# Fused image network with a deformable convolution: two of nine taps of image 1 sampled densely on TensorE instead of gathered

## The reference, cut to what matters

```python
y0 = jnp.floor(y); x0 = jnp.floor(x)      # y, x: base position of the tap plus its offset
val = w00 * gather(y0i, x0i) + w01 * gather(y0i, x1i) + w10 * gather(y1i, x0i) + w11 * gather(y1i, x1i)
val = val * msk                            # zero outside the image
out = jnp.einsum('op,bphw->bohw', weight, col)   # 32 outputs from 9 taps x 32 channels
```

## Time and profile before

| what | us |
|---|---|
| median of 3 runs | 1137.83 |
| lowest, highest | 1137.09, 1138.41 |
| span of the profiled execution | 1135.9 |
| GpSimd busy, of which gathers | 672.6, of which 580.6 |
| VectorE, TensorE, ScalarE busy | 706.4, 680.0, 225.3 |
| first gather of image 1 starts | 748.85 |
| last gather starts | 1120.69 |

### The profile page before, as it was taken

The page is one execution under the profiler, slowest core; times in us unless marked ns, Lnnn a source line. Parts: engine busy times, 40 slices in busy tenths (PEclk is TensorE's granted clock), DMA queues, the critical chain, the costliest instruction groups (busy, mean ns, idle before and its releaser), DMA issues.

```text
span 1135.9 us, 7902 instructions
## 1 busy us (share of the span) xinstructions
PE 680.0 (60%) x2301; PEld 408.8 (36%) x2301; DVE 706.4 (62%) x906; ACT 225.3 (20%) x296; POOL 672.6 (59%) x620
## 2 busy tenths in 40 slices
PE   3347667778777967788888868634343433334343
PEld 1123222223221444444444424634343433334343
DVE  4989717899995887999999985632323223232322
ACT  1120267544532641121212101000000000000000
POOL 0000000776630787777777777777777777777773
PEclk9668979799996956777777776555555555555555
DMA  4000142000007211211111136221111111111121
GB/s 109 0 1 0 28 106 47 0 1 0 1 0 157 57 36 51 54 50 50 52 49 52 50 92 167 65 54 51 51 51 51 51 51 50 51 49 52 50 67 31
DMA packets 24234, 56.34 MB, mean 50 GB/s; under 512 B 12016, under 2 KB 12400, under 8 KB 23088
## 3 DMA queue, kind: packets, MB, share of 16 engines
q0 software_dynamic: 18432, 37.79, 12.4%
q1 hardware_dynamic: 4912, 15.60, 6.0%
q10 hardware_dynamic: 864, 2.64, 1.0%
HBM read 42.36 MB, written 5.24 MB: 42 GB/s over the span
## 4 chain that ended last, share of the span: by engine, by line
POOL 51%; issue 20%; DVE 10%; PE 3%; DMA 1%; POOLq 0%; ACT 0%; ACTq 0%; DVEq 0%
POOL got L742 50%; DVE scratch L1093 5%; DVE scratch L1100 3%; PE PS L976 1%; DMA G<-XN 1%; PE PS L1193 1%; PE PS L969 1%; PE PS L961 1%; PE PS L776 0%; ACT scratch L1051 0%; DVE st L132 0%; DVE X L1134 0%; DMA got<-corner_table,idx_slot 0%; POOL scratch L1069 0%; ACTq L1158 0%
## 5 line engine op out<-in xcount | busy, mean ns | idle before, releaser
L742 POOL DMA_INDIRECT got<-corner_table,idx_slot x486 | 483.9, 996 | 148.2 <-issue 148.2
L776 PE MATMUL PS<-ln_g,w 128*128 128x32 f32 x1152 | 231.5, 373 | 0.0
L776 PEld LDWEIGHTS PS<-ln_g,w 128*128 128x128 f32 x1152 | 226.8, 302 | 0.0
L750 DVE COPY idx_slot<-idx_all 128x9 uint32 (+1 forms) x64 | 11.7, 182 | 292.9 <-DMA got<-corner_table,idx_slot 244.9
L774 PE MATMUL PS<-UZ,mat 128*128 (+1 forms) x64 | 20.2, 408 | 230.2 <-DVE ln_g L763 230.2
L976 PE MATMUL PS<-scratch,wt 128*128 128x512 f32 x256 | 147.3, 706 | 0.5 <-DVE scratch L1100 0.5
L961 PE MATMUL PS<-parts,selb 96*128 96x512 bf16 (+1 forms) x256 | 90.2, 454 | 81.4 <-DVE scratch L1019 41.5
L742 POOL DMA_INDIRECT got<-corner_table,idx_all x90 | 96.7, 1074 | 65.2 <-DVE prime L1267 38.0
L774 PEld LDWEIGHTS PS<-UZ,mat 128*128 128x128 f32 x64 | 16.0, 311 | 234.3 <-issue 227.2
L1331 POOL MEMSET w<- 128x1152 f32 x1 | 1.1, 1058 | 157.4 <-POOLq L593 157.4
L753 DVE TENSOR_TENSOR prodg<-got,coef 128x1152 f32<-128x1152 f32 x64 | 86.8, 1356 | 0.3
(11 more groups left out here) (307 smaller groups left out, 959.8 us busy)
## 6 DMA issues: line engine op xcount, KB each, us to landing
got<-corner_table,idx_slot POOLq DMA_INDIRECT x486, 2.5
XN<-ln_g SPq DMA_DIRECT2D x6, 256.0 KB, 5.1
got<-corner_table,idx_all POOLq DMA_INDIRECT x90, 2.5
corner_table<-scratch SPq DMA_DIRECT2D x1, 1056.0 KB, 10.3
corner_table<-XN SPq DMA_DIRECT2D x1, 1056.0 KB, 10.4
X<-in_x SPq DMA_DIRECT2D x4, 256.0 KB, 4.9
corner_table<-scratch SPq DMA_DIRECT2D x1, 992.0 KB, 8.2
corner_table<-XN SPq DMA_DIRECT2D x1, 992.0 KB, 8.4
```

The source lines that it names most:

```text
L742: pool.indirect_dma_start(got[:, slot, tap, :, :].rearrange("p k c -> p (k c)"), None, tables[b], bass.IndirectOffsetOnAxis(ap=index[:, ta ...
L776: last = nc.tensor.matmul(group_psum(slot), w3[:, t, :], colgs[slot][:, t * C:t * C + C], start=False, stop=(t == TAPS - 1))
```

## The change

Image 1 gathers only taps 0 to 6 (`NEAR` = 7). Taps 7 and 8 (`DENSE` = 2) are computed by dense interpolation in 16 batches: one for each tap, each quarter of the image and each half of it (512 pixels). Image 0 is as before. In a batch:
- SP loads rows of positions and of masked block selectors from DRAM, broadcast over partitions (`dense_load`, five DMAs, 1 MB in all, two buffers).
- ScalarE makes the hat in y (Abs, Relu) and five ramps in x (Relu with a knot) of 512 columns (`dense_scalar`), one batch ahead.
- VectorE multiplies each ramp, cut at 1, by the hat (`dense_weights`, five instructions).
- TensorE multiplies the five by the image's differences from column to column (`dense_sample`, 2 x 5 products of 512 columns), VectorE selects the block of columns by a mask while it reads PSUM (`dense_pick`, two instructions), and TensorE applies the tap's weights and sums (`dense_sum`, two products).

The batches stand behind turns 30, 32, ... 60 on VectorE, TensorE and ScalarE; picks and sums follow one batch later. `dense_add` adds the sums of a half to the residual. `dense_fields` (in image 1's preparation, behind the reciprocal) and `dense_table` (behind it) are new work of VectorE, the four iotas of GpSimd come at the start. The loops of five turns on TensorE, ScalarE and VectorE are unrolled; GpSimd's loop stays. Image 0 is now stored in one piece behind the loads of batch 3, and image 1's stores wait for `dense_add`.

```diff
+DENSE = 2
+NEAR = TAPS - DENSE
+SLOPES = 5
@@ group_gather, group_weigh
-            for tap in range(TAPS):
+            for tap in range(NEAR if b else TAPS):
...
-            v.wait_ge(gathered[slot], uses * (16 * TAPS) + 16 * TAPS)
+            v.wait_ge(gathered[slot], arrived)
...
-            tell(v, nc.vector.tensor_tensor(prodg[:, :, :, :].rearrange("p t k c -> p (t k) c"),
+            tell(v, nc.vector.tensor_tensor(prodg[:, 0:n, :, :].rearrange("p t k c -> p (t k) c"),
...
@@ prepare, vector
                 vchain(v, nc.vector.reciprocal(msk, msk))
+                if b == 1:
+                    dense_fields(v)
@@ new functions
+        def dense_fields(v):
...
+            vchain(v, nc.vector.memset(fields[:, :, 10 * DENSE:], 0.0))
+            vchain(v, nc.vector.tensor_scalar(blk, x, 0.125, 0.5, ALU.mult, ALU.subtract))
...
+            for k in range(8):
+                vchain(v, nc.vector.scalar_tensor_tensor(row(2 + k), blk, float(k), msk, ALU.is_equal, ALU.mult))
+            nc.vector.transpose(fields_t, fields[:, :, :].rearrange("p g k -> p (g k)")).then_inc(de["rows_out"], 1)
+
+        def dense_table(v):
...
+            for j in range(4):
+                last = nc.vector.tensor_tensor(steps_odd[up, j, :, :], tab[up, 2 * j + 1:W:8, 0, :], tab[up, 2 * j:W:8, 0, :], ALU.subtract)
+            last.then_inc(de["steps_out"], 1)
+            nc.vector.tensor_copy(steps[up, 0, :, :], tab[up, 0:W:8, 0, :])
+            for j in range(1, 4):
+                nc.vector.tensor_tensor(steps[up, j, :, :], tab[up, 2 * j:W:8, 0, :], tab[up, 2 * j - 1:W:8, 0, :], ALU.subtract)
...
+        def dense_load(sp, n):
+            half, q, d = BATCHES[n]
+            k, cols = n % 2, slice(half * BANK, (half + 1) * BANK)
+            if n >= 2:
+                sp.wait_ge(de["ramps"], 6 * (n - 1))
+                sp.wait_ge(de["t_used"], 2 * (n - 1))
+            sp.dma_start(loads[k][:, 0:2, :], rows_dram[q, 10 * d:10 * d + 2, cols].partition_broadcast(P)).then_inc(load[k], 16)
+            for i in range(4):
+                sp.dma_start(loads[k][32 * i:32 * i + 32, 2:4, :],
+                             rows_dram[q, 10 * d + 2 + i:10 * d + 10:4, cols].partition_broadcast(32)).then_inc(load[k], 16)
+
+        def dense_scalar(act, n):
...
+            act.wait_ge(load[k], 80 * (n // 2 + 1))
+            if n >= 2:
+                act.wait_ge(de["t_psum"], 2 * (n - 1))
+            nc.scalar.activation(hats[k], loads[k][:, 0, :], ACT.Abs, bias=negy[:, 0:1]).then_inc(de["absd"], 1)
+            nc.scalar.activation(ramps[k][:, 0, :], loads[k][:, 1, :], ACT.Relu, bias=knot[:, 0:1]).then_inc(de["ramps"], 1)
+            act.wait_ge(de["absd"], n + 1)
+            nc.scalar.activation(hats[k], hats[k], ACT.Relu, bias=1.0, scale=-1.0).then_inc(de["ramps"], 1)
+            for j in range(1, SLOPES):
...
+                nc.scalar.activation(ramps[k][rows, j, :], loads[k][rows, 1, :], ACT.Relu, bias=knot[rows, j:j + 1]).then_inc(de["ramps"], 1)
+
+        def dense_weights(v, n):
...
+            for j in range(SLOPES):
+                rows = up if j == SLOPES - 1 else slice(0, P)
+                v.wait_ge(de["ramps"], 6 * n + 2 + j)
+                nc.vector.scalar_tensor_tensor(ramps[k][rows, j, :], ramps[k][rows, j, :], 1.0, hats[k][rows, :],
+                                               ALU.min, ALU.mult).then_inc(de["prods"], 1)
+
+        def dense_sample(pe, n):
...
+                pe.wait_ge(de["t_used"], max(2 * (n - 1), 1))
+            for h in range(2):
+                for j in range(SLOPES):
...
+                    last = nc.tensor.matmul(PS[:, 2 * k + h, :], steps[rows, j, 4 * h:4 * h + 4, :].rearrange("p b c -> p (b c)"),
+                                            ramps[k][rows, j, :], start=(j == 0), stop=(j == SLOPES - 1))
+                last.then_inc(de["t_psum"], 1)
+
+        def dense_pick(v, n):
...
+            for h in range(2):
+                v.wait_ge(de["t_psum"], 2 * n + h + 1)
+                nc.vector.tensor_tensor(picked[:, h, :], PS[:, 2 * k + h, :], loads[k][:, 2 + h, :], ALU.mult).then_inc(de["t_used"], 1)
+
+        def dense_sum(pe, n):
...
+                last = nc.tensor.matmul(PS[32 * q:32 * q + 32, 4 + half, :], w3_rows[:, d, :], picked[:, h, :],
+                                        start=(d == 0 and h == 0), stop=(d == DENSE - 1 and h == 1))
...
+        def dense_add(v, half):
...
+            v.wait_ge(de["sum_psum"], LAST_BATCH[half] + 1)
...
+            nc.vector.tensor_tensor(resids[1][:, cols], resids[1][:, cols], PS[:, 4 + half, :], ALU.add).then_inc(de["added"], 1)
...
+        FIRST_TURN, LAST_TURN = 30, 62
+
+        def batches_after(G):
+            return [n for n in range(len(BATCHES)) if FIRST_TURN + n * (LAST_TURN - FIRST_TURN) // len(BATCHES) == G]
@@ SP
+                dense_first(sp)
+                for n in range(len(BATCHES)):
+                    if n == 4:
+                        store(sp, 0, 0, GROUPS)
+                    dense_load(sp, n)
+                sp.wait_ge(de["added"], 2)
+                store(sp, 1, 0, EARLY)
+                store(sp, 1, EARLY, GROUPS)
@@ VectorE
                 prep[1][3](v, lambda k: vector_turn(v, IN_PREPARE + k))
-                for G in range(IN_PREPARE + 3, REST):
+                dense_table(v)
+                for G in range(IN_PREPARE + 3, B * GROUPS):
                     vector_turn(v, G)
-                with nc.vector.Fori(0, (B * GROUPS - REST) // SLOTS) as i:
...
+                    for n in batches_after(G):
+                        dense_weights(v, n)
+                        if n:
+                            dense_pick(v, n - 1)
+                        if n - 1 == LAST_BATCH[1]:
+                            dense_add(v, 1)
+                    if G == LAST_TURN:
+                        dense_pick(v, len(BATCHES) - 1)
+                        dense_add(v, 0)
```

More of the change, by code:

```diff
@@ L771, in group_multiply @@
         def group_multiply(pe, b, G, g, slot):
+            n = NEAR if b else TAPS
             pe.wait_ge(l3["col_done"], G + 1)
@@ L774, in group_multiply @@
             nc.tensor.matmul(group_psum(slot), ident, group_pixels(b, g), start=True, stop=False)
-            for t in range(TAPS):
-                last = nc.tensor.matmul(group_psum(slot), w3[:, t, :], colgs[slot][:, t * C:t * C + C], start=False, stop=(t == TAPS - 1))
+            for t in range(n):
+                last = nc.tensor.matmul(group_psum(slot), w3[:, t, :], colgs[slot][:, t * C:t * C + C], start=False, stop=(t == n - 1))
             last.then_inc(l3["o_psum"], 1)
```

144 lines of the change are left out of this document (111 added, 33 removed).

## The result

The changed kernel takes **1051.6 us** (median of 4 runs, 1048.4 to 1053.6) beside 1137.5 (4 runs); the ratio is 0.924 (0.922 to 0.926).

A forecast was written before the change was run, and what follows sets the result against it. GpSimd's gather issue was taken to bound image 1. -80 - 2.5 + 37 + 3 - 1.4 = -44 us against the 1135.9 span gave 1092, plus 1.9 around the span 1094 us; range 1055 to 1112.

The forecast's parts named there:

- What bounds it: Image 1 is paced by how often GpSimd can issue gathers, 1.296 us each; the other engines have room.
- -80 for the gathers: Image 1's GpSimd queue: 64 gathers fewer at 1.25 us each, all on the path, save 80 us.
- +37: Batches: VectorE's five back-to-back weight instructions hold a gather 2.3 us per batch, 37 us over 16 batches.
- Rival (a): GpSimd isn't held in the batches, since VectorE meets each ramp as it comes, with gaps: 1057 us; chance 0.20.
- -2.5 for the surplus: Image 1's gather time over 1.25 us each, 13 us in all, shrinks by 2.5 us as VectorE's turn instructions shorten.
- +3 for `dense_table` and `dense_fields`: Their new VectorE instructions hold gathers about 2.5 us (`dense_table`) and 0.5 us (`dense_fields`).
- Tail -1.4: End of the kernel: VectorE's last-turn instructions shorter by 0.5 us, TensorE's small products by 0.9 us.
- TensorE: Batches of 21 or 10.3 us by clock; a slot takes 18 us at worst, fits under 18.3, costs nothing.
- rival (c): Slower than before: TensorE stays at 1.2 GHz in the batches, 28 us a slot, 1208 us; chance 0.04.
- Loads: Each batch's 1 MB in five DMAs takes 9 us (5 to 14), covered, ramps ready before VectorE asks.
- (b): The batch's own loop of picks, load, activations and weights paces; needs loads over 13.6 us; 1120 us; chance 0.13.
- the other edits: New preparation work, iotas, moved stores and dense_add: 3 us from `dense_table` and `dense_fields`, the rest covered.

The follow-up runs named there:

- e8: Changed kernel without four of the ten interpolating products of each batch (ramps 1 and 3): 1050.5 us.
- e6: Changed kernel without VectorE's five weight instructions per batch; TensorE reads the ramps without the hats: 1049.4 us.
- e2: Changed kernel with image 1's four additions as scalar_tensor_tensor of 1024 elements and the batch weights in three instructions of 1024, 1024 and 512: 1050.2 us.
- e12: Changed kernel with image 1's four additions reading and writing the tile scratch alone: 1052.4 us (one run).
- e18: Changed kernel with the batches' ramps in the tile XN instead of scratch, the hats staying in scratch: 1050.8 us.
- e13: Changed kernel with image 1's product of the taps over all nine taps, though seven are gathered: 1056.8 us.
- e1: Changed kernel with image 1's additions as eight tensor_tensor of 512 and the batch weights as tensor_tensor without the cut at 1: 1047.5 us (one run).
- e16: Changed kernel with image 0's product of nine taps split into eight taps and one, with no stop between: 1053.3 us.
- e11: Changed kernel with one wait ahead of the five batch weights instead of one at each: 1051.3 us (one run).
- e20: Changed kernel with four extra additions of 128x1024, issued without stops, in seven turns of image 1: 1058.6 us (one run).
- e10: Changed kernel where VectorE waits for the end of each of image 1's four additions before issuing the next: 1046.6 us.
- e15: Changed kernel with waits between image 1's four additions and dense_add(1) one batch later: 1046.0 us.
- e17: Changed kernel with waits between image 1's additions, dense_add(1) one batch later, and image 0's product split into eight taps and one: 1047.8 us.
- a0_again: The changed kernel measured once more, nothing edited: 1049.8 us, ratio to before 0.9217.
- e4: Changed kernel without anything dense; taps 7 and 8 of image 1 are left out of the result: 1044.3 us.
- e14: Changed kernel loading only the first two of the 16 batches' rows, which all batches use: 1045.2 us.

## Why the prediction was wrong, step by step

- **What bounds it: right.** GpSimd's queue of gathers bounded image 1 and still does; e8 and e6 take 32 us of TensorE and 45 of VectorE (131.73 to 86.16 in 760 to 1000) away and gain nothing.
- **-80 for the gathers: right**, 79.6 measured.
- **+37, the step that failed**: "What follows when such instructions stand back to back is in one row". From the 6.98 us beside four L817 it was taken that a gather is held to the end of any such stretch. Measured: 1.6 us for all 16 batches. The trace of before has one more case that goes with it (the gather at 397.04 lasts 2.30 us, through a copy and L753), but 6.98 us was a single row, and it carried the largest term after the -80, for a mechanism that turns out to need something more. The argument that `dense_weights` "is built the same" was true of operation, length and tiles (e2, e12 and e18 make them the same) and didn't help. Rival (a), GpSimd isn't held, is what happened, by its own mark (no gather of the stretch over 1.7 us: the longest is 1.64). Its reason was wrong too: it had VectorE meet each ramp as it comes, with gaps, but the ramps were ready, and gathers got in at the end of the second instruction, where there is no gap.
- **-2.5 for the surplus: a term mis-sized**, and it is why even (a)'s 1057 is 5 us too high. Outside the batches' own 1.6 us the holds fell by 13.4 - 3.8 = 9.6. The rows had most of what was needed: in a quiet turn the next gather starts 1.1 us into L753 and asks 0.13 us later, so an instruction of 1.36 us catches it each turn and one of 7/9 of that does not. I scaled the surplus, where it had to be placed. The quiet turn was not typical, though: in image 1 before the change the next gather came 0.90 us into L753 (median), where even the short product would catch it; that it comes at 1.11 with seven gathers was in no row.
- **+3 for `dense_table` and `dense_fields`: not there.** Gathers beside them (716 to 726 and 730 to 734 us) last 0.94 to 1.00. The small ones of `dense_table` are back to back too, and let gathers in.
- **Tail -1.4: 2.4.** L784 to L791 and L808 (3.17 us in place of 4.03) shrank as told.
- **TensorE: right in kind.** The ten products took 9.4 to 12.3 us, the clock 0.89, so rival (c) is out: it had the clock stay at its lower level, and it did not. **Loads: shorter** than the 9 us. One DMA lands 3.6 or 4.5 us after its issue (medians), all five of a batch 6.6 to 7.5 us after the first issue (7.7 and 9.4 for the first two batches). VectorE waited for ramps once, 5.0 us before the first batch, so (b) is out. What the loads do cost was not seen at all: they make gathered data late, 2.0 us of holds and at most 4.6 us of time.

The sum by measured terms, -79.6 - 8.0 - 0.9 - 0.3 - 2.4 = -91.2, with +2.0 for the start, is what the profiles show. Of the 45.6 us between 1094 and the profiled 1048.4, the term of +37 makes 35.4, the surplus about 7, the other edits 4, the tail 1, and the late start takes 2 back.

By the Trainium skill ("SBUF — State Buffer", Who interferes with whom) a `tensor_tensor` was seen not to stall the descriptor generation of DMAs, which gave 1057 us. The batches' five come near to that (1.6 us in all), but they are `scalar_tensor_tensor`; L784 is a `tensor_tensor` and held 32 gathers in e13, and beside e1's eight one lasted 7.26 us. The same page (SBUF: two separate sides) says that of a VectorE instruction with two SBUF inputs and a GpSimd one that reads SBUF, whichever starts first has the shared pair of ports for the whole instruction. The holds that end with one instruction agree with it, the 6.98 us don't follow from it.

## What to carry to other kernels

When a queue of short operations sets the end, look at where each stands against the other engine's instructions, not at their mean: 0.27 us more of one instruction brought 4 us of holds over 32 turns, since its end passed the point at which a gather asks, and moving another boundary (e16) brought 4 us as well. A term that rests on one extreme row should be held against the other places where VectorE's instructions follow without a stop, and until something shows why that row differs, the ordinary hold of one instruction is the likelier price. And loads that are ready in time can still cost: they make other transfers late, on which the path does wait.

## What the runs showed of the hardware

- A gather is held by a VectorE instruction with two SBUF inputs as if it asked 0.13 us after its start, and is then let in mostly at the end of the instruction that runs, whether or not the next follows without a stop (15 gathers in the batches, 16 in e11, and in e16 and e20).
- One place refuses: beside image 1's additions a gather is held for 4.6 to 6.3 us in every kernel without stops there, over all boundaries between the additions. With a stop of 35 ns it is let in at the first of them (2.23 us in e10 and e15, 2.24 in e17). Kind, length, tiles of the operands and of the indices, and the run itself moved elsewhere do not explain it; the cause is open.
- The spread between profiled executions is made of such holds too. The stretch ahead of image 1 runs the same instructions in after, a0_again, e4 (all but `dense_fields` and `dense_table`), e6, e8, e11, e14 and e18 and took 382.1 to 385.2 us, with summed holds of 22.5 to 25.6. Stretch less holds is 359.6 to 359.7 us in all twenty profiles, e13's 386.8 and e16's 386.3 included.
